# Splitting all pairs of the second experts' second layer, on one core

## The reference

```
x = x + 0.5 * experts(layernorm(x))
x = x + attention_and_mlp(layernorm(x))
x = x + 0.5 * experts(layernorm(x))
```

```
h = relu(buf_e @ w1 + b1)      # 256 x 256 rows, hidden size 1024
y = h @ w2 + b2                # back to 256
```

## Time and profile before

| what | value |
|---|---|
| median of 3 runs | 722.16 us (721.7 to 723.1) |
| the profiled execution | 722.26 us |
| its span | 720.5 us |
| mean granted clock of TensorE | 0.973 |
| TensorE busy | 668.8 us (93%) |
| VectorE busy | 492.3 us (68%) |
| ScalarE busy | 421.0 us (58%) |
| GpSimd busy | 336.3 us (47%) |

### The profile page before, as it was taken

One profiled execution on the slowest core, in us unless ns is written; L12 is line 12 of the kernel. 1 busy time (PEld: TensorE's weight loads), 2 busy tenths in 40 slices (PEclk: granted clock), 3 DMA queues, 4 the chain that ended last, 5 costly groups with the idle time before them and its releaser, 6 DMA issues.

```text
span 720.5 us, 17429 instructions
## 1 busy us (share of the span) xinstructions
PE 668.8 (93%) x6214; PEld 574.6 (80%) x6214; DVE 492.3 (68%) x1332; ACT 421.0 (58%) x841; POOL 336.3 (47%) x513
## 2 busy tenths in 40 slices
PE   7689999998788999999999999999999985999897
PEld 5449999974566889898888888988978763999896
DVE  7856757525688777878878778878675475776562
ACT  5756546412334767676767766767654642767552
POOL 5234574122133563645574765846537463353322
PEclk9869999999999999999999999999999996999999
DMA  8479788404766544544465565555534243567640
GB/s 262 151 235 337 220 272 280 150 30 99 114 104 104 98 69 89 97 87 68 96 95 114 89 88 126 79 99 89 91 69 130 84 145 98 154 217 224 183 141 29
DMA packets 285183, 95.56 MB, mean 133 GB/s; under 512 B 213988, under 2 KB 282176, under 8 KB 285098
## 3 DMA queue, kind: packets, MB, share of 16 engines
q1 hardware_dynamic: 269418, 82.85, 47.7%
q0 software_dynamic: 4800, 10.95, 5.5%
q10 hardware_dynamic: 10880, 0.66, 1.0%
HBM read 65.09 MB, written 29.40 MB: 131 GB/s over the span
## 4 chain that ended last, share of the span: by engine, by line
PE 71%; DVE 11%; issue 6%; POOL 5%; ACT 4%; ACTq 1%; DMA 1%; POOLq 0%; SPq 0%; DVEq 0%
PE bank L1777 65%; PE bank L1786 7%; POOL hids L817 2%; DVE kv_ L1731 1%; DVE den L1609 1%; DVE att_ L1607 1%; ACT feats L1026 1%; DVE hn_ L1648 1%; ACT feats L1028 1%; ACTq L394 1%; DMA x_all<-in_L_attn_q_x_dram 1%; POOL sth L803 1%; POOL stz L795 1%; DVE stz L1745 0%; DVE hnts L1626 0%
## 5 line engine op out<-in xcount | busy, mean ns | idle before, releaser
L1777 PE MATMUL bank<-down_w,hids 128*128 128x256 f32 x768 | 103.9, 284 | 1.8 <-POOL hids L817 1.6
L1777 PE MATMUL bank<-hnts,up_w 128*128 128x512 f32 x384 | 104.8, 408 | 0.1
L1777 PEld LDWEIGHTS bank<-down_w,hids 128*128 128x128 f32 x768 | 96.3, 188 | 4.8 <-POOL hids L817 3.1
L817 POOL TENSOR_TENSOR hids<-hid,hids 128x512 fp32r<-128x512 f32 x64 | 82.7, 1292 | 36.9 <-ACT hids L1071 36.9
L1777 PE MATMUL bank<-qkv_w,xnts 128*128 128x256 f32 (+1 forms) x384 | 76.8, 347 | 5.7 <-DVE xnts L1620 5.2
L1777 PEld LDWEIGHTS bank<-qkv_w,xnts 128*128 128x128 f32 x384 | 60.5, 189 | 22.8 <-DVE xnts L1620 7.9
L1777 PEld LDWEIGHTS bank<-hnts,up_w 128*128 128x128 f32 x384 | 67.5, 189 | 11.7 <-ACT hids L1071 0.3
L1068 ACT ACTIVATE hid<-bank,cols 128x512 f32<-128x512 f32 x64 | 44.0, 688 | 40.0 <-PE bank L1777 39.7
L792 POOL TENSOR_SCALAR stz<-stz 128x1 f32<-128x1 f32 x32 | 7.6, 236 | 126.4 <-DVE stz L1632 126.4
L1777 PE MATMUL bank<-a_w,xa_h 128*128 128x256 f32 x256 | 60.2, 379 | 0.0
L1777 PE MATMUL bank<-xa_xt,a_w 128*128 128x256 f32 x384 | 55.1, 294 | 1.4 <-DVE xa_xt L1358 1.4
(11 more groups left out here) (273 smaller groups left out, 1570.2 us busy)
## 6 DMA issues: line engine op xcount, KB each, us to landing
qkv_rows<-feats SPq DMA_DIRECT2D x32, 384.0 KB, 2.7
a_raw<-in_L_ffn_w_dram SPq DMA_DIRECT2D x32, 256.0 KB, 4.3
a_w<-in_L_ffn_w_dram SPq DMA_DIRECT2D x32, 256.0 KB, 3.7
b_raw<-in_L_ffn_w_dram SPq DMA_DIRECT2D x32, 256.0 KB, 3.6
b_w<-in_L_ffn_w_dram SPq DMA_DIRECT2D x32, 256.0 KB, 3.1
mid_rows<-x_all SPq DMA_DIRECT2D x8, 512.0 KB, 2.9
values<-qkv_rows SPq DMA_DIRECT2D x32, 128.0 KB, 2.9
late_rows<-x_ SPq DMA_DIRECT2D x8, 512.0 KB, 3.1
```

What stands on the lines that cost most here:

```text
L817: pool.tensor_tensor(hids[1][u % 3][:], hid[u % 2][:], f32(hids[0][u % 3][:]), ALU.subtract).then_inc(s_hidl, 1)
L1777: return pe.matmul(dst, left, right, start=start, stop=stop, skip_group_check=True)
```

## The change

In the second experts all four pairs of the second layer are split, for x = 8 to 14; the last expert keeps two split pairs. `split_of(x)` gives the number per expert. For the new pairs 2 and 3, ScalarE makes the high parts of w2 and of the hidden activations and VectorE the low part of w2, in the loops where they made those of pairs 0 and 1. The low part of the hidden activations of pairs 2 and 3 is made by GpSimd (`low_hidden` in its block), in iteration u for pair u - 1, ahead of the root, the sends and the gathers of that iteration. The split parts of w2 (32 KB a partition) and of the hidden activations (16 KB) are no longer in stage b's own buffers but over the middle's weights `qkv_w`, `o_w`, `up_w` and `down_w` (48 KB together), so stage b's other buffers that follow them lie 24 KB lower.

```diff
+        with ExitStack() as late:
+
+            b_w2p = list(zip(*(tiles(late, f"b_w2p{x}", 2, [P, KE, D], F32R) for x in range(2))))
+            b_hs = [tiles(late, f"xb_hs{b}", PAIRS, [P, 2, CAP], F32R) for b in range(2)]
...
-            split = SPLIT if second else 0
-            w2p = [tiles(stack, f"{name}_w2p{b}", 2, [P, 2 * SPLIT, D], F32R) for b in range(2)] if second else None
-            hs = [tiles(stack, f"{n}_hs{b}", SPLIT, [P, 2, CAP], F32R) for b in range(2)] if second else None
+            w2p, hs = (b_w2p, b_hs) if second else (None, None)
...
-        SPLIT = 2
+        BY_DVE = 2
+
+        def split_of(x):
+
+            return 0 if x < E else BY_DVE if x == 2 * E - 1 else PAIRS
+
+        def splits_before(x):
+
+            return sum(split_of(i) for i in range(x))
...
+        def hidden_low(x, j):
+
+            if j < BY_DVE:
+                return expert_sems.hlow, (x - E) * BY_DVE + j + 1
+            return s_hidl, NG * KM + (x - E) * (PAIRS - BY_DVE) + j - BY_DVE + 1
...
-                if x > ex.first and c < ex.split:
+                if x > ex.first and c < split_of(x - 1):
...
+            def low_hidden(u, ex):
+                j = u % PAIRS
+                pool.wait_ge(ex.sem.relu, relus_made(u, True))
+                pool.tensor_tensor(ex.buf.hs[1][j][:], ex.buf.h[u % 4][:], f32(ex.buf.hs[0][j][:]),
+                                   ALU.subtract).then_inc(s_hidl, 1)
+
...
+                    if u > ex.first * PAIRS and (u - 1) // PAIRS < ex.end and BY_DVE <= (u - 1) % PAIRS < split_of((u - 1) // PAIRS):
+                        low_hidden(u - 1, ex)
                     if j == 0 and ex.first < x < ex.end - 1:
                         root_rows(x + 1, ex)
...
-                if c < ex.split:
+                if c < split_of(x):
                     act.wait_ge(ex.sem.got2[c], 16 * (x + 1))
...
-                if j < ex.split:
+                if j < split_of(x):
                     act.wait_ge(ex.sem.relu, relus_made(u, False))
...
-                if c < ex.split:
+                if c < split_of(x):
                     pair = slice(2 * c, 2 * c + 2)
...
-                    if u > ex.first * PAIRS and (u - 1) // PAIRS < ex.end and (u - 1) % PAIRS < ex.split:
+                    if u > ex.first * PAIRS and (u - 1) // PAIRS < ex.end and (u - 1) % PAIRS < min(split_of((u - 1) // PAIRS), BY_DVE):
                         low_hidden(u - 1, ex)
...
-                if j < ex.split:
+                if j < split_of(x):
                     pe.wait_ge(ex.sem.low1, parts_made(x, j, True))
-                    pe.wait_ge(ex.sem.hlow, (x - ex.first) * ex.split + j + 1)
+                    pe.wait_ge(*hidden_low(x, j))
```

More of the change, by code:

```diff
@@ L24 @@
                                       "got1 got2 high1 low1 hlow biased")
-Experts = namedtuple("Experts", "slots source target first end raw w1s w2s buf sem split w2p")
+Experts = namedtuple("Experts", "slots source target first end raw w1s w2s buf sem w2p")
 def build(nc, x_in, ln1_w, ln1_b, wq, bq, wk, bk, wv, bv, wo, bo, ln2_w, ln2_b,
@@ L189, in experts @@
                 fin=tiles(stack, f"{n}_fin", 4, [P, D]), hs=hs)
-            return Experts(slots, source, target, second * E, (second + 1) * E, raw, w1s, w2s, buf, expert_sems, split, w2p)
-        SPLIT = 2
+            return Experts(slots, source, target, second * E, (second + 1) * E, raw, w1s, w2s, buf, expert_sems, w2p)
+        BY_DVE = 2
[3 more added lines that the diff above has]
+            return sum(split_of(i) for i in range(x))
         def parts_made(x, c, second):
-            return x * PAIRS + max(x - E, 0) * SPLIT + c + (min(c, SPLIT) if x >= E else 0) + 1 + second
+            return x * PAIRS + splits_before(x) + c + min(c, split_of(x)) + 1 + second
         def relus_made(u, whole):
             x, j = divmod(u, PAIRS)
-            split = max(x - E, 0) * SPLIT + (min(j + whole, SPLIT) if x >= E else 0)
-            return 2 * (u + 1) + split
+            return 2 * (u + 1) + splits_before(x) + min(j + whole, split_of(x))
+        def hidden_low(x, j):
+            if j < BY_DVE:
+                return expert_sems.hlow, (x - E) * BY_DVE + j + 1
+            return s_hidl, NG * KM + (x - E) * (PAIRS - BY_DVE) + j - BY_DVE + 1
         with ExitStack() as phase:
@@ L810, in residual, with low_mid @@
                 pool.tensor_tensor(xr[n % 9][:], x1[n % 8][:], xo[n % 3][:], ALU.add).then_inc(s_xr, 1)
-            def low_hidden(g, m):
+            def low_mid(g, m):
                 u = g * KM + m
@@ L827, in _ @@
                 if 0 <= g_up < NG:
-                    low_hidden(g_up, 2 * j_up)
+                    low_mid(g_up, 2 * j_up)
                 if s == 20:
@@ L845, in _ @@
                 if 0 <= g_up < NG:
-                    low_hidden(g_up, 2 * j_up + 1)
+                    low_mid(g_up, 2 * j_up + 1)
                 if s == MID_STEPS - 3:
```

## The result

The kernel with the change takes **740.31 us** (median of 4 runs, 738.13 to 740.80) against 722.63 before (4 runs): a ratio of 1.0238 with a 95% interval of 1.0218 to 1.0258, +17.7 us. The forecast was +8.3. The profiled execution took 740.15 with a span of 738.2, so its rows are worth the median to 0.2 us.

What follows compares the result with a forecast made beforehand. TensorE bounded the kernel before; with the change GpSimd's queue ahead of its new parts would decide. Terms 0.6 + 0.2 + 3.8 + 3.8 + 0.5 - 0.56 = +8.3 us on 722.16 gave 730.5 us, range 725 to 736.5.

Steps and rivals of the forecast that it cites:

- Split pairs on TensorE: Down and up products, seven experts: each pair turned from whole to split saves 0.28 us, 3.92 us in all.
- End of the middle: Expert 8's new parts in the middle's last steps: one VectorE subtraction on an unbroken chain adds 0.6 us (0 to 1.3).
- Expert 8: Period without indirect DMAs ahead of its parts: VectorE sets it at 12.6 us, +0.2 (bounds -0.56 and +1.5).
- GpSimd's queue, experts 9 to 11: Low parts behind sends and gathers: loop 12.6 us plus VectorE's lateness 1.1, period 13.7; 3 x 1.28 = +3.8 us.
- Expert 12, the drain: Pair 2's low part stands behind GpSimd's drain: period 18.6 us against 14.80, +3.8 (bounds +0.7 and +5.1).
- Expert 13 and the clock: Period after the drain's stall: half clock's 1.46 us stays, VectorE is behind; 14.4 us, +0.5.
- 3 x 1.46: Rival: stalls in experts 9, 10 and 11 each bring the half clock, +4.4 us, 734.9 us; chance 0.17.
- The port: VectorE beside GpSimd's subtractions: 0.62 us lost for each of two, 12.6 us an expert; 13.9 by the skill's rule.
- Expert 14: Period with neither a gather's DMAs nor a drain: 0.56 us shorter.
- slower by less: Rival: port costs nothing, VectorE on time, GpSimd's loop and the drain remain; +3.1, 725.3 us; chance 0.15.
- Faster: Rival: drain and port both cheap, drain tail 2.8 us, no half clock after it; 720.8 us; chance 0.06.
- no change: Rival: drain and port both cheap, but the half clock after the drain stays; 722.3 us; chance 0.05.

Runs made afterwards that it cites:

- a_three: The changed kernel with three split pairs per expert, all low parts on VectorE, gathers behind the root, drain behind expert 13's sends: 717.06 us.
- a_idle: The changed kernel with unused TensorE products ahead of the wait of down pair 2 in experts 9, 11 and 12: 733.91 us.
- b_subs: The kernel before with 14 more GpSimd subtractions on old weights at the change's queue places, results read by nothing: 731.29 us.
- a_alldve: The changed kernel with VectorE making all four low parts, none on GpSimd: 732.52 us.
- a_gather: The changed kernel with second experts' gathers behind both low parts and the root, drain behind expert 14's last low part: 726.91 us.

## Why the prediction was wrong

The sign, the bound ("the queue in front of its new parts") and the place of every gap were right; the size was half. By its own steps:

- **Split pairs on TensorE.** Right: 624.83, 626.27, 627.69 are the 1.44 and 1.42 forecast, and a_three shows the 0.28 per pair whole.
- **End of the middle.** Right, +0.60, to be read from one wait (1.88 to 2.48).
- **Expert 8.** Right, 12.64 for 12.6.
- **GpSimd's queue, experts 9 to 11.** This step failed: 3 x 1.28 = 3.8 forecast, 11.7 measured. From down pair 3 of expert 8 to that of expert 9 (627.69 to 646.42) the loop took 18.73 us where the sum had 13.7. The finish began 3.77 us after the first (the sum had 2.7 to 3.1). The four DMAs were taken as fixed at 6.55; they were 8.26, and 8.24 in expert 11 (1.7 more each time, cause open). The gap was priced by its length alone; behind it TensorE lost another 2.40 us, and 1.58 in expert 11. The step also said that VectorE's 1.16 for the root "is VectorE's own round trip". With the root behind two parts in the same queue it became 4.27. In the kernel after this wait was not the last one: the finish behind it waited 2.37 us more (1.44 in expert 11), which in a_idle, where TensorE keeps its clock, it does not. b_subs (13.9 with no reader) shows that the root's loop alone would hold a longer period, and a_alldve (13.40 with no GpSimd part) that it does so with long DMAs; a_gather shows that the order in the queue opens it.
- **Expert 12, the drain.** The gap of 6.56 is within the forecast 6 to 7. The period was 20.72 for 18.6: the half clock behind the gap, 2.15, is the whole difference.
- **Expert 13 and the clock.** I placed the clock's cost in expert 13, where it had been. It moved with the gap: the whole 1.46 left expert 13 (12.46), which now runs at full speed, and three larger ones came. For the long gap 1.46 stood in the sum and 2.15 came; for those of experts 9 and 11 nothing stood there and 3.98 came. That was only a rival ("3 x 1.46", chance 0.17), because the gaps were forecast at 1 to 2 us; at 3.5 us they were far above the 1.9 that had cost 1.46 before. So this error follows from the one on the queue. a_idle shows the clock as the cause: it takes back 4.8 of the 6.1 in the periods.
- **The port.** The 0.62 us from one collision was too small. That row had a single GpSimd subtraction, which had run for 0.5 us before VectorE's began. The change issues two in a row, and VectorE loses the sum of both and more: 3.29 - 0.69 = 2.6 us, and 2.9 in a_gather. Twice 1.30 is what should have stood in VectorE's sum: 11.3 + 2.6 = 13.9 is the period that a_gather has, where a loss larger by 0.3 meets other work smaller by 0.3 (9.85 us for 10.15), so the match to 0.1 is in part luck. The Trainium skill (SBUF — State Buffer, Who interferes with whom) has the two exclude each other for the whole instruction; the prediction's 13.9 us by that rule is the 13.88 to 13.91 measured once the queue was out of the way. In the kernel after, the stretched rows add up to 1.0 us in expert 8, 2.6 in expert 10, 2.0 in expert 13 and 2.1 in expert 14, and to nothing in experts 9, 11 and 12. So the port is not what made the bad periods long; how much of VectorE's lateness at their start came from the 1.0 us in expert 8 is not separated.
- **Expert 14.** -0.56 forecast, +0.07 measured: at 720.13 TensorE waits 0.40 for GpSimd's part again.

The rival "slower by less" (the port costs nothing) missed the DMAs and the clock like the forecast, and the one that had the clock, at 734.9 us, missed the longer DMAs. "Faster" and "no change" needed a drain tail under 4 us and a clock without a price; neither came near.

## What to carry to other kernels

Before work is put on an engine that has slack on average, write out its queue in program order around the new item, and price everything that then stands behind it, not only the new reader: here a root of 0.96 us behind two parts cost 8.7 us with nothing reading the parts (b_subs), of 17.7 in all. Where two engines wait for each other once per period, lateness can feed itself once the slack (here 0.98 us) is used up, the more so where the work in the loop grows as well (here the DMAs, from 5.22 to 8.50 us). Add to each gap what TensorE loses behind it (here 1.6 to 2.4 us for a gap of 3.5), and try the order of the queue before the amount of work: moving the gathers and the drain was worth 12 to 13 us here, the split pairs 3.9.

## What the hardware showed that was not expected

- A drain removed is not a drain saved: 7.48 us at the program's end for 3.00, in both kernels without it. Placed where GpSimd has time it cost nothing (718.30 for 722.47).
- A VectorE operation that meets two back-to-back GpSimd subtractions ends only behind both: 3.29 and 3.79 us for rows of 0.69 and 0.87.
- Indirect sends of the same shape take 1.10 us in some periods and 2.2 to 2.3 in others. Two trials to bring the slow kind about failed; its cause is open.
- Products that nobody reads, set into three gaps, made the kernel 5 to 6 us faster than without them.
